# Projecting the first keys of a masked cross attention earlier, and issuing the small weight loads later

## The reference, cut to what matters

```python
x = x + L0_xattn(ln(x), ctx)        # one head, 1601 context tokens a batch
x = x + L0_attn(ln(x))              # causal self attention, 16 heads of 8
x = x + L0_ffn(ln(x))               # 8 gated experts, top 2
x = x + L1_xattn(ln(x), ctx, mask)  # masked cross attention, self attention, FFN
x = x + L1_attn(ln(x), key, value)  # fake-quantised attention
x = x + L1_ffn(ln(x))               # 8 experts, top 2

# in L1_xattn:
q, k, v = heads(x @ cq_w + cq_b), heads(ctx @ ck_w + ck_b), heads(ctx @ cv_w + cv_b)
scores = einsum('bqhd,bkhd->bhqk', q, k) / sqrt(8) + mask
ca = einsum('bhqk,bkhd->bqhd', softmax(scores), v)
x = layer_norm(ca @ co_w + co_b + input) * co_g + co_be
# the other layers' bodies are not touched
```

## Time and profile before

| | |
|---|---|
| time, median of 3 runs | 1282.2 us |
| the profiled execution | 1281.95 us, span 1280.2 us, granted clock 0.889 of full |
| PE / DVE / ACT / POOL busy | 80% / 51% / 38% / 15% of the span |
| DMA | 98.52 MB, mean 77 GB/s |

### The profile page before, as it was taken

One profiled execution on the slowest core, in us unless ns is written; L12 is line 12 of the kernel. 1 busy time (PEld: TensorE's weight loads), 2 busy tenths in 40 slices (PEclk: granted clock), 3 DMA queues, 4 the chain that ended last, 5 costly groups with the idle time before them and its releaser, 6 DMA issues.

```text
span 1280.2 us, 22033 instructions
## 1 busy us (share of the span) xinstructions
PE 1022.1 (80%) x9278; PEld 731.4 (57%) x9278; DVE 657.4 (51%) x1131; ACT 483.0 (38%) x622; POOL 196.8 (15%) x178
## 2 busy tenths in 40 slices
PE   3687777899873699999999999999658634848888
PEld 2355456787761266666666666666436412547776
DVE  4133655343343556666666676664166367763111
ACT  0234332222232146666666656666304200402333
POOL 2000430211212001111111111110141013200110
PEclk9799887999996579999999999999877766859999
DMA  8585000101201333333333333330000100001110
GB/s 278 187 314 207 2 1 1 50 25 43 83 0 53 141 123 108 111 130 110 107 107 108 139 137 123 108 108 18 1 1 2 33 0 1 2 0 34 34 33 17
DMA packets 41349, 98.52 MB, mean 77 GB/s; under 512 B 9976, under 2 KB 24960, under 8 KB 41264
## 3 DMA queue, kind: packets, MB, share of 16 engines
q1 hardware_dynamic: 41264, 97.29, 22.1%
HBM read 55.50 MB, written 0.73 MB: 44 GB/s over the span
## 4 chain that ended last, share of the span: by engine, by line
PE 61%; DVE 16%; ACT 8%; issue 5%; SPq 4%; DMA 3%; POOL 3%; DVEq 0%; POOLq 0%; ACTq 0%
PE PS L264 57%; DVE kl L1493 3%; ACT kh L1081 3%; ACT PT L1094 3%; DVE prT L1497 2%; SPq L896 2%; PE PS L357 2%; DVE mx L1508 2%; DMA ctxT<-in_ctx_T 1%; PE PS L294 1%; POOL rstd_all L283 1%; DVE x L667 1%; DVE u_all L277 1%; DMA work_area<-in_ctx_T 1%; DVE stats_all L269 1%
## 5 line engine op out<-in xcount | busy, mean ns | idle before, releaser
L1508 DVE TENSOR_REDUCE mx<-PS 128x2 f32<-128x1024 f32 x192 | 230.7, 1217 | 85.1 <-PE PS L264 85.0
L1094 ACT ACTIVATE PT<-PS 128x1024 f32<-128x1024 f32 (+1 forms) x208 | 212.4, 1021 | 95.2 <-PE PS L264 94.0
L264 PE MATMUL PS<-QB,QS 128*128 128x512 f32 x576 | 159.4, 425 | 23.7 <-DVE wcol L655 21.7
L264 PE MATMUL PS<-QB,KS 128*128 128x256 f32 (+1 forms) x832 | 166.8, 323 | 9.2 <-ACT PT L1094 8.5
L264 PEld LDWEIGHTS PS<-QB,QS 128*128 128x128 f32 x576 | 110.3, 202 | 60.7 <-issue 26.8
L264 PEld LDWEIGHTS PS<-QB,KS 128*128 128x128 f32 (+1 forms) x832 | 116.5, 187 | 43.5 <-issue 31.8
L264 PE MATMUL PS<-PT,work_area 128*32 128x128 f32 (+1 forms) x3328 | 135.3, 281 | 0.5 <-ACT PT L1094 0.5
L264 PE MATMUL PS<-KS,QB 64*128 64x512 f32 (+1 forms) x512 | 110.8, 462 | 13.1 <-DMA KS<-kl 9.5
L667 DVE SCALAR_TENSOR_TENSOR x<-PS,wcol,x 128x128 f32<-128x128 f32 x128 | 44.9, 351 | 138.1 <-PE PS L264 134.7
L264 PE MATMUL PS<-nat_area,work_area 128*128 128x128 f32 (+2 forms) x1312 | 100.8, 261 | 17.2 <-DVE work_area L662 5.9
L264 PEld LDWEIGHTS PS<-nat_area,work_area 128*64 128x64 f32 (+1 forms) x1312 | 96.3, 165 | 31.3 <-ACT work_area L395 12.3
(11 more groups left out here) (237 smaller groups left out, 1255.5 us busy)
## 6 DMA issues: line engine op xcount, KB each, us to landing
KS<-kh SPq DMA_DIRECT2D x32, 800.5 KB
ctxT<-in_ctx_T SPq DMA_DIRECT2D x24, 800.5 KB, 4.4
nat_area<-in_ctx_tiles SPq DMA_DIRECT2D x16, 832.0 KB, 6.6
KS<-kl SPq DMA_DIRECT2D x16, 800.5 KB
work_area<-in_ctx_T SPq DMA_DIRECT2D x8, 800.5 KB, 10.2
nat_area<-in_L_ffn_experts_w SPq DMA_DIRECT2D x24, 256.0 KB, 3.3
nat_area<-in_L_ffn_W SPq DMA_DIRECT2D x16, 256.0 KB, 3.0
KS<-mask_parts SPq DMA_DIRECT2D x32, 50.1 KB
```

What stands on the lines that cost most here:

```text
L264: return T.matmul(o, l, r, start=start, stop=stop, **k)
L1094: P["exp_a"].done(S.activation(PT[0:rows, par, :], PS[0:rows, 1024:2048], ACT.Exp), f"e{k}")
L1508: ins = V.reduce_max(by_pair[:, :, j // 3, j % 3:j % 3 + 1], src, AX)
```

## The change

1. Of the small loads, seven (`SECOND`: the four weights of the first self attention, the router of its experts and the two quantised weights) are issued two at a time behind `load_values` of pairs 2 to 5. The other 43 are issued behind the first expert weights (`first_contexts`), under a counter of their own, `later_weights_loaded`; all engines that use them wait for it before the expert loop. Then SP waits for the end of the first self attention, whose tiles share `ctxT`, and loads the contexts of batches 0 and 1.
2. The keys of batches 0 and 1 are computed in the expert loop: a quarter of each (401 columns, `KW`) a round, behind h(1,0) and h(3,0), in banks 6 and 7. Batch 1 gets its own halves in `nat_area`. Their stacks are copied before the loop is over (`stack_keys`).
3. Behind the loop TensorE computes the values of batch 0 at once. The first 128 tokens (batches 0 and 1) are normalised, transposed, projected, split and stacked by themselves, then come the maxima of batch 0 and the first three of batch 1 (slots -2 and -1, which hold nothing else now), and then the other 896 tokens. The queries' halves have their own tiles (`q_hi`, and `QB2` for the low part).
4. GpSimd computes the layer norm's `rstd` before it fills the ones of the values and fills only these columns; it also adds `co_b`, which VectorE did.

```diff
+        SECOND = [w for w in WLOADS if w[0] in [W[n] for n in ("L0_attn_W_Q", "L0_attn_W_K", "L0_attn_W_V", "L0_attn_W_o",
+                                                               "L0_ffn_gate", "L1_attn_in_w", "L1_attn_out_w")]]
+        WLOADS = [w for w in WLOADS if w not in SECOND]
+        N_W, N_LATER = len(SECOND), len(WLOADS) + 16
+        KW = 401
+        def early_keys_tensor(b, i):
+            T.wait_ge(ctxT_loaded[b], 16)
+            P["pk_p"].done(mm(bank(6 + b, KW), W["L1_xattn_ck_w"][:, :], ctxT[:, b, bass.ds((KW - 1) * i, KW)]), f"b{b}")
+        def early_keys_scalar(b, i):
+            at(S, "pk_p", f"b{b}", i)
+            P["pk_a"].done(S.activation(KH[b][:, bass.ds((KW - 1) * i, KW)], bank(6 + b, KW), ACT.Identity,
+                                        bias=COLS["L1_xattn_ck_b"][:, 0:1]), f"b{b}")
+        def early_keys_vector(b, i):
+            at(V, "pk_a", f"b{b}", i)
+            P["pk_v"].done(V.scalar_tensor_tensor(KL[b][:, bass.ds((KW - 1) * i, KW)], bank(6 + b, KW),
+                                                  COLS["L1_xattn_ck_b"][:, 0:1], KH[b][:, bass.ds((KW - 1) * i, KW)],
+                                                  ALU.add, ALU.subtract), f"b{b}")
+        def early_keys(keys, i):
+            return {(1, 0): lambda: keys(0, i), (3, 0): lambda: keys(1, i)}
 # SP
             load_values(1)
-            for t, src in WLOADS:
-                dst = t[:, :, :] if len(t.shape) == 3 else t[:, :]
-                sp.dma_start(dst, src).then_inc(loads, 16)
...
                 load_values(n)
+                for t, src in SECOND[2 * (n - 2):2 * (n - 1)]:
+                    load_weight(t, src, loads)
             at(sp, "cc_p", "pc", PAIRS - 1)
+            def first_contexts():
+                for t, src in WLOADS:
+                    load_weight(t, src, later_loads)
...
+                at(sp, "a0_p", "y")
+                for b in range(2):
+                    load_context(b)
-            at(sp, "q3_v", "ql")
-            sp.wait_ge(stacks_ready, 4)
+            for b in range(2):
+                stack_keys(b)
+            at(sp, "q3_v", "ql0")
+            sp.wait_ge(stacks_ready, 3)
             for k, src in enumerate((qh, ql, qh)):
-                sp.dma_start(QS[k:128:4, :, :].bitcast(F32), src.bitcast(F32)).then_inc(qs_stacked, 16)
+                sp.dma_start(QS[k:128:4, :, 0:128].bitcast(F32), src[:, 0:128].bitcast(F32)).then_inc(qs_first, 16)
 # GpSimd
-            G.memset(VA[0], 1.0).then_inc(consts_ready, 1)
-            G.memset(VA[1], 1.0).then_inc(consts_ready, 1)
             ln_all_gpsimd(3)
+            for va in VA:
+                G.memset(va[:, :, :, 16:32], 1.0).then_inc(consts_ready, 1)
...
+            slot(-2)
+            slot(-1)
+            g.wait_ge(ln_T, 8)
+            G.tensor_tensor(u_all[:, :, :], u_all[:, :, :], rows_of("L1_xattn_co_b"), ALU.add).then_inc(co_biased, 1)
 # VectorE (TensorE alike)
+            ln_stats_vector(3, x)
+            ln_apply_vector(x, u_all, range(3))
+            at(V, "q3_p", "T0")
+            P["q3_v"].done(V.tensor_copy(xT_all[:, 0:128], bank(6, 128)), "x0")
+            ln_apply_vector(x, u_all, range(3, 5))
+            queries(0, 0, 128, bank(0, 128), prT[:, 512:640])
+            ln_apply_vector(x, u_all, range(5, PAIRS))
+            slot(-2)
+            slot(-1)
+            V.wait_ge(ln_T, 7)
+            V.tensor_copy(xT_all[:, 128:512], bank(7, 384)).then_inc(ln_xT, 1)
+            V.wait_ge(ln_T, 8)
+            V.tensor_copy(xT_all[:, 512:1024], bank(6)).then_inc(ln_xT, 1)
+            queries(1, 128, 512, bank(7, 384), prT[:, 512:896])
+            queries(2, 512, 1024, bank(6), prT[:, 512:1024])
             slots(slot)
```

More of the change, by code:

```diff
@@ L104, in build @@
         tok_w = sb("tok_w", [128, PAIRS, EXPERTS])
+        small_at = nc.sbuf_base
         mask_at = nc.sbuf_base
@@ L275, in ln_all_vector, with ln_apply_vector @@
             V.wait_ge(ln_rstd, r + 1)
-            for t in range(PAIRS):
+        def ln_apply_vector(src, dst, tiles):
+            for t in tiles:
                 V.tensor_scalar(dst[:, t, :], src[:, t, :], mv_all[:, t, 0:1], rstd_all[:, t:t + 1],
                                 ALU.subtract, ALU.mult).then_inc(ln_xn, 1)
+        def ln_all_vector(r, src, dst):
+            ln_stats_vector(r, src)
+            ln_apply_vector(src, dst, range(PAIRS))
             V.wait_ge(ln_xn, PAIRS * (r + 1))
@@ L651, in moe_scalar, with moe_vector @@
                 beside.get((n, c), lambda: None)()
-        def moe_vector(name, gated, i, first=lambda: None):
+        def moe_vector(name, gated, i, first=lambda: None, beside={}):
             for j in range(2):
@@ L663, in moe_vector @@
                                                             bank(2 * (c % 2) + 1), ALU.mult), step_name("h", n, c))
+                    beside.get((n, c), lambda: None)()
                     continue
@@ L711, in build @@
         T_loaded = [sem(f"T_loaded{q}") for q in range(2)]
-        progress("q3_p", ["q0", "q1"])
-        progress("q3_v", ["qf0", "qf1", "qh", "ql"])
+        progress("q3_p", ["T0", "q0", "q1", "q2"])
+        progress("q3_v", ["x0"] + [f"{part}{j}" for j in range(3) for part in ("qf", "qh", "ql")])
+        progress("pk_p", ["b0", "b1"])
+        progress("pk_a", ["b0", "b1"])
+        progress("pk_v", ["b0", "b1"])
         CS = range(len(CHUNKS))
@@ L807, in sides @@
         def sides(n, k):
+            if n < 0:
+                return [item for item in SIDES[k] if item == "nm" and n == -1]
             return [item for item in SIDES[k]
@@ L822, in bank7_free @@
         def bank7_free(n, k):
-            before = [(m, item) for m in range(-2, n + 1) for i in range(KT) for item in closed(sides(m, i))
+            before = [(m, item) for m in range(n + 1) for i in range(KT) for item in closed(sides(m, i))
                       if (m, i) < (n, k) and item != "nm"]
+            if not before:
+                at(nc.tensor, "q3_v", "ql1")
             if before:
@@ L975, in slot @@
                 if b < BATCH:
+                    if b == 2:
+                        g.wait_ge(qs_stacked, 16 * 3)
                     if b >= 3:
@@ L1287, in slot @@
                             pe.wait_ge(nm_stacked, 32 * (n + 1))
+                        if n == 0 and k == 1:
+                            at(T, "q3_v", "ql2")
                         if k >= 1:
@@ L1309, in slot @@
                         maximum(b, j)
+            slot(-2)
+            slot(-1)
+            pe.wait_ge(ln_xn, 4 * PAIRS)
+            for t in range(1, 4):
+                last = T.transpose(PS[:, 3584 + 128 * (t - 1):3584 + 128 * t], u_all[:, t, :], ident)
+            last.then_inc(ln_T, 1)
+            for t in range(4, 8):
+                last = T.transpose(PS[:, 3072 + 128 * (t - 4):3200 + 128 * (t - 4)], u_all[:, t, :], ident)
+            last.then_inc(ln_T, 1)
+            pe.wait_ge(ln_xT, 7)
+            P["q3_p"].done(mm(bank(7, 384), W["L1_xattn_cq_w"][:, :], xT_all[:, 128:512]), "q1")
+            pe.wait_ge(ln_xT, 8)
+            P["q3_p"].done(mm(bank(6), W["L1_xattn_cq_w"][:, :], xT_all[:, 512:1024]), "q2")
             slots(slot)
```

147 lines of the change are left out of this document (91 added, 56 removed).

## The result

The changed kernel takes **1237.75 us** (median of 4 runs, 1236.87 to 1245.12) beside 1281.39 of the kernel before: a ratio of **0.9672** [0.9625, 0.9719]. The forecast was 1247 with a range of 1240 to 1262. The profiled execution took 1236.87 us, its span 1235.0.

The account below looks back on a forecast made before the run. TensorE bounds the expert loop and slot 0; context loads bound part of the first cross attention, one dependency chain the stretch behind the loop. 1281.95 - 9.0 + 7.0 - 32.8 gave 1247 us, range 1240 to 1262.

Parts of the forecast that it names:

- The way behind the loop: From the expert loop's end to slot 0's probabilities: 42.3 us instead of 75.1, a gain of 32.8, between 28 and 35.
- "all behind them" the same: Stages behind slots 0 to 16: same instructions on the same data, so no change in time was put in the sum.
- first cross attention: Stage ahead of the first self attention: moving the small loads away gains 9.0 us, between 5 and 11.
- The cycle: First cross attention: keys land 11.1 us after a pair's sums, which end 8.9 us behind the start of its scores.
- The price of 1.1 us for the seven loads: First cross attention: weights put back between contexts delay the next keys by at most two 0.46 us issues, for three pairs.
- the whole row, 0.88: Expert loop: each of eight added 401-column key matmuls costs TensorE 0.88 us at full clock, 7.0 in all.
- hand-off: Expert loop: ScalarE and VectorE work per early key hides behind TensorE; otherwise up to 1.2 us x 8; loop-pays-more rival 0.11.
- the register addresses: Expert loop: addresses from a register, new on TensorE, cost between nothing and 0.3 us each; nothing was taken.
- "I keep this for a copy an eighth as large": Behind the loop: the first queries' copy into their stack still takes 6.0 us, lower end 4.5.
- The two projections "at the lower clock": Ahead of slot 0: first copy 0.6 us, then TensorE's 384 and 512 columns take 1.56 and 2.07 us.
- the bias: Ahead of slot 0: GpSimd's bias addition may stretch VectorE's query split, delaying slot 0's second step 1.6 us; not summed.
- the rival of a lasting low clock: Slots: TensorE stays at 1.2 GHz, some 24 us more per slot, 1295 us with two slots; chance 0.03.

Follow-up runs that it names:

- second_early: Changed kernel with all seven weight loads of the first self attention issued together behind pair 2's keys: 1237.91 us, 0.9675 of the kernel before.
- both_moves: Changed kernel with GpSimd's two fills moved behind the queries' second spread and the seven weight loads together behind pair 2's keys: 1236.61 us, 0.9684 of the kernel before.
- keys_split: Changed kernel with late fills, seven loads together behind pair 2's keys, and context 1's early keys moved behind the loop: 1232.54 us, 0.9632 of the kernel before.
- qs_full: Changed kernel with late fills and the queries' first copy at all 1,024 columns instead of 128: 6.44 us from first issue to spread; no kernel time given.
- keys_behind: Changed kernel with the eight early key matmuls, activations and differences behind the expert loop instead of in it: 1248.39 us, 0.9762 of the kernel before.

## Why the forecast missed

The parts gained and paid where the forecast said; their sizes were off, and one term had been put at nothing. Two steps took the time below the range. The way behind the loop gained 3.4 us more than forecast, above all because the queries' copy was kept at 6.0 us and took 3.2. And "all behind them" the same, which stood for 0, was 3.9 us shorter. The loop (2.2) and slot 0 (0.8) add to these; the largest single error, 4.5 us in the first cross attention, pulls the other way and hid part of them. The rest is the base (item 6). Means over the profiles that share the code of the stage, 3 or 4 of the order before and 7 to 13 of the changed one:

| term | forecast | measured |
|---|---|---|
| first cross attention | -9.0 (5 to 11) | -4.5 (97.7 to 93.2) |
| loop | +7.0 | +4.8 (174.6 to 179.4) |
| the way | -32.8 | -36.2 (75.8 to 39.6) |
| slot 0 to slot 1 | 0 | -0.8 (31.6 to 30.8) |
| all behind the last slot | 0 | -3.9 (362.9 to 359.0) |

1. **First cross attention: half of its size, below its own lower end.** The cycle had 11.1 us from a pair's sums to the landing of keys each time; for pair 5 it was 12.9, and scores(5) then took 4.61 us at the lower clock in place of 2.92. The price of 1.1 us for the seven loads was too small: the three stretches from sums to scores that `second_early` shows are together 2.2 us shorter than the changed kernel's. That does not clearly reach the stage: without the loads X was 88.4, 91.8 and 93.1 (`second_early`, `both_moves`, `keys_split`), beside 91.2 to 96.2, a mean of 93.2, in eleven profiles of the changed order of loads. Why pair 5's keys take 12.0 to 12.4 us even without them stays open.
2. **Loop: right in kind, 7.0 a little high.** The added busy time is 5.5 us (163.43 less 157.94). That is 0.69 us for a key; the forecast had the whole row, 0.88, although it said itself that the engine is free before its row ends. Its lower end of 5.9 is nearly the 5.5, and the doubled keys cost 4.3. No hand-off shows, and no price for the register addresses.
3. **Behind the loop: the step that failed.** "I keep this for a copy an eighth as large": 6.0 us, with a lower end of 4.5; it was 3.2, below the end. `qs_full` shows that its size is the cause. In `keys_behind`, issued behind larger copies, the same copy took 7.3. The two projections "at the lower clock", 4.3 us from the last maxima to slot 0: it was 2.8. The clock was the lower one, 0.51, as forecast; but from the first projection to slot 0 it was 2.31 us and not 1.56 + 2.07, since the forecast again added whole rows, and slot 0's first row starts before the last projection's ends (413.44 + 2.87 = 416.31, against 415.75). Against these stand 2.4 us of a contention that the forecast did not see, though it had read the rows of both operations. For the bias, where it did look, its case did not arise: GpSimd's addition took 2.34 us and ended at 415.61, and VectorE's steps from SBUF to SBUF began at 415.77. Beside it ran only two copies out of PSUM (0.55 and 0.68).
4. **Slots: right.** From slot 1 to the last it is 429.3 to 429.8 us in 15 of 18 profiles, of both kernels and their variants, and 431.2 at most. Slot 0's clock was 1.00 and not 0.89; the rival of a lasting low clock did not come. Slot 0's wait of 1.19 us comes of its early start: the last query part was ready at E + 41.4, sooner than the 44.4 forecast, but slot 0 itself came 3.9 us sooner.
5. **"All behind them the same": the instructions were, the time was not.** A1 alone is 3.6 us shorter at 0.80 for 0.75 (63.8 for 67.4). What in the changed order brings that about stays open. The range had no room for this term.
6. **The base.** The profiled 1281.95 lies above what the kernel before takes in the later runs (1278.1 to 1279.3). So 3 of the 9 us between 1247 and 1238 are the base and no part of the change: by medians of these runs it gives about 40 us, by the profiles 45.

The table sums to -40.6, which the 40 by medians agrees with.

## What to carry to other kernels

A copy whose size changes gets a new time, from its bytes; do not carry the old one along, and look at what stands ahead of it in the queue. A matmul added to a full engine costs the time until the next one starts, which is less than its row (0.69 us for a row of 0.84 here). Look for contention at each place where a GpSimd operation now runs beside a VectorE operation that works out of SBUF, also where the change only takes a wait away and so moves two old operations side by side. And let the range have a term of some microseconds for untouched stages that run at a mixed clock: they are shifted by every change ahead of them.

## What the hardware showed beside

VectorE's scale and shift of one 128x128 tile out of SBUF went from 0.29 to 1.07 us beside a GpSimd fill of SBUF (0.86 and 3.21 for three), while maxima read from PSUM took 13.67 us for twelve with and without it. And the same 488 matmuls of the second self attention took 63.2 to 69.9 us in 18 profiles, at granted clocks of 0.83 to 0.73, with no more than a pause of 8 us ahead of them between 67.4 and 63.2. A copy of 128 columns into the stack took 3.2 us from its first issue to its user, one of 1,024 columns 6.4, and the small one 7.3 with larger copies issued just ahead of it.
